# Cross attention and a mixture of experts: the first expert step in a new order, a token's rows by lower and higher expert, and products that nobody reads

## The reference

```python
x = x + cross_attention(layernorm(x), ctx, ctx, mask, Wq, bq, Wk, bk, Wv, bv, Wo, bo)   # 16 heads of 16
# flat: the 1792 rows (16 x 112) of layernorm(x), 256 wide
gate_probs = softmax(flat @ router_w)                       # 8 experts
topk_w, topk_idx = top_k(gate_probs, 2); topk_w /= topk_w.sum()
cw = zeros(T, 8).at[arange(T), topk_idx].add(topk_w)
h = silu(einsum('td,edf->etf', flat, w1))                   # 256 -> 512
y = einsum('etf,efd->etd', h, w2)                           # 512 -> 256
x = x + einsum('etd,te->td', y, cw)
```

## Time and profile before

| | |
|---|---|
| median of 3 runs | 491.9 us (490.89 to 492.44) |
| profiled execution | 491.83 us, its span 490.1 us |
| PE, DVE, ACT, POOL busy | 85%, 71%, 54%, 47% of the span |
| mean granted clock of TensorE | 0.917 |
| expert steps, first transposition to last output product | 326.6 to 465.9 |

### The profile page before, as it was taken

The page is one execution under the profiler, slowest core; times in us unless marked ns, Lnnn a source line. Parts: engine busy times, 40 slices in busy tenths (PEclk is TensorE's granted clock), DMA queues, the critical chain, the costliest instruction groups (busy, mean ns, idle before and its releaser), DMA issues.

```text
span 490.1 us, 10668 instructions
## 1 busy us (share of the span) xinstructions
PE 414.3 (85%) x4155; PEld 383.4 (78%) x4155; DVE 345.7 (71%) x703; ACT 266.4 (54%) x350; POOL 232.4 (47%) x263
## 2 busy tenths in 40 slices
PE   2475679999999999999999999637989999999800
PEld 2364557999999989999988988537989999999800
DVE  2785466887877878887787858854686666666427
ACT  3231226567566666557663453526767777777500
POOL 8352343422333222332222374753676888886443
PEclk9796689999999999999999997558999999999965
DMA  7949838777777778877641039912222222332157
GB/s 174 229 132 230 269 117 166 155 160 162 155 161 161 159 133 170 177 160 145 144 101 34 26 108 379 327 54 55 66 86 66 87 87 87 87 88 74 47 211 267
DMA packets 58323, 69.83 MB, mean 142 GB/s; under 512 B 19073, under 2 KB 51602, under 8 KB 58274
## 3 DMA queue, kind: packets, MB, share of 16 engines
q1 hardware_dynamic: 52338, 56.30, 47.5%
q0 software_dynamic: 4032, 11.02, 7.6%
q10 hardware_dynamic: 1904, 1.84, 1.1%
HBM read 35.64 MB, written 14.78 MB: 103 GB/s over the span
## 4 chain that ended last, share of the span: by engine, by line
PE 74%; DVE 11%; issue 5%; DMA 4%; ACT 3%; POOL 2%; DVEq 0%; SPq 0%; ACTq 0%; POOLq 0%
PE ps L1467 38%; PE ps L1528 11%; PE ps L1543 9%; PE ps L1557 8%; DVE x L1457 2%; PE ps L1817 2%; PE ps L1570 1%; DVE x_rows_sb L1100 1%; DVE neg_max L1053 1%; DMA y_back<-y_rows 1%; PE ps L1636 1%; DVE h_lo L1384 1%; PE ps L1638 1%; ACT h_hi L982 1%; DMA keep<-keep_scratch 1%
## 5 line engine op out<-in xcount | busy, mean ns | idle before, releaser
L1053 DVE TENSOR_REDUCE neg_max<-ps 112x1 f32<-112x376 f32 x256 | 133.7, 546 | 38.2 <-PE ps L1528 33.6
L830 ACT ACTIVATE probs<-ps 125x1344 f32<-125x1344 f32 x64 | 82.7, 1292 | 42.9 <-PE ps L1543 37.7
L1528 PE MATMUL ps<-k_stack,q_stack 98*112 98x376 f32 x256 | 88.1, 378 | 11.0 <-issue 6.5
L589 POOL TENSOR_TENSOR k_lo<-k_f,k_hi 128x752 fp32r<-128x752 f32 x16 | 28.8, 1801 | 120.2 <-ACT k_hi L804 117.7
L1528 PEld LDWEIGHTS ps<-k_stack,q_stack 98*112 98x112 f32 x256 | 45.2, 178 | 24.8 <-DVE neg_max L1053 14.0
L748 POOL DMA_INDIRECT rows<-xn_rows,token_of_row x42 | 53.9, 1284 | 20.6 <-issue 12.2
L756 POOL DMA_INDIRECT y_rows<-y_out,slot_of_row x42 | 45.3, 1078 | 33.4 <-ACT y_out L996 23.3
L1543 PE MATMUL ps<-q_stack,k_stack 100*125 100x224 f32 x384 | 52.8, 273 | 0.4 <-ACT probs L830 0.3
L1467 PE MATMUL ps<-flat_t_hi,w_hi 128*128 128x256 f32 x168 | 48.7, 290 | 4.5 <-DVE flat_t_lo L1362 4.5
L1543 PEld LDWEIGHTS ps<-q_stack,k_stack 100*125 100x125 f32 x384 | 50.5, 188 | 1.5 <-ACT probs L830 1.0
L1467 PE MATMUL ps<-w_hi,h_hi 128*128 128x256 f32 x168 | 48.6, 289 | 3.0 <-issue 1.6
(11 more groups left out here) (200 smaller groups left out, 1011.9 us busy)
## 6 DMA issues: line engine op xcount, KB each, us to landing
k_stack<-k_hi SPq DMA_DIRECT2D x64, 188.0 KB, 4.5
w_all<-w SPq DMA_DIRECT2D x2, 4096.0 KB, 18.0
k_stack<-k_lo SPq DMA_DIRECT2D x32, 188.0 KB, 5.5
ctx_raw<-ctx_t SPq DMA_DIRECT2D x32, 187.5 KB, 5.3
q_stack<-q_scratch SPq DMA_DIRECT2D x32, 168.0 KB
q_scratch<-q_hi SPq DMA_DIRECT2D x16, 224.0 KB, 3.1
y_back<-y_rows SPq DMA_DIRECT2D x7, 512.0 KB, 6.6
q_scratch<-q_lo SPq DMA_DIRECT2D x8, 224.0 KB, 2.8
```

The source lines that it names most:

```text
L589: pool.tensor_tensor(kl[:, :, :], kf[:, :, :], kh[:, :, :].bitcast(F32), ALU.subtract)\
L830: act.activation(pf[j % 2][:, :, :], ps[0:CT, BK_ST:BK_ST + KT, 0:4 * S], ACT.Exp).then_inc(pf_ready, 1)
L1053: dve.tensor_reduce(neg_max[:, s:s + 1], ps[0:S, BK_MAX + s % 2, 0:CP], AX.X, ALU.max, negate=True).then_inc(max_read, 1)
L1528: pe.matmul(ps[0:S, BK_MAX + a, 0:CP], qs[b.ring][0:R_MAX, q, S * a:S * (a + 1)], ks[b.ring][0:R_MAX, q, :], start=True, stop=True).then_i ...
```

## The change

In the planning, `chosen[:, 0]` becomes the expert with the lower number of a token's two, `chosen[:, 1]` the other. In the tail, outputs are loaded back in two halves: those of the lower experts once all steps but the last have been scattered (and the last `w1_low` is done, since they lie where `w1_all` was), then those of the higher experts; each half is seven transfers of 256 KB in pieces of 1 KB. DVE makes all 28 sums, POOL none. On ACT, `silu` splits in `silu` and `silu_high`, and the order in a step becomes silu(t), rows_high(t+1), silu_high(t), w2_high(t), copy_y(t-1), w1_high(t+2); a Silu of one column stands behind the gates' Exp. The first step has an order of its own on ACT, DVE and PE. PE makes 24 products into a bank that nobody reads ahead of the first transposition and 8 behind it.

```diff
+BK_SPIN = 3
...
-        y_back = sb("y_back", [P, NT, TOP, D])
+        y_back = sb("y_back", [P, TOP, NT, D])
...
-            for p in range(2):
-                sp.wait_ge(y_scattered[p], 32 * ((STEPS - p + 1) // 2))
-            for g in range(NTG):
-                sp.dma_start(y_back[:, 2 * g:2 * g + 2, :, :],
-                             y_rows[TOP + TOP * TG * g:TOP + TOP * TG * (g + 1), :]
-                             .rearrange("(n p c) d -> p n c d", p=P, c=TOP)).then_inc(y_in[g], 16)
+            def load_outputs(c):
+
+                steps_done = STEPS - 1 + c
+                for p in range(2):
+                    sp.wait_ge(y_scattered[p], 32 * ((steps_done - p + 1) // 2))
+                if c == 0:
+                    sp.wait_ge(w1l_ready, STEPS)
+                for g in range(NTG):
+                    sp.dma_start(y_back[:, c, 2 * g:2 * g + 2, :],
+                                 y_rows[TOP + TOP * TG * g:TOP + TOP * TG * (g + 1), :]
+                                 .rearrange("(n p c) d -> p c n d", p=P, c=TOP)[:, c, :, :]).then_inc(y_in[c][g], 16)
...
             def silu(t):
                 act.wait_ge(h_done, t.n + 1)
-
                 if not early(t, 2):
                     act.wait_ge(hl_ready, t.n - 1)
+                act.activation(hf[t.par][:, :, :], silu_source(t), ACT.Silu).then_inc(hf_ready, 1)
+
+            def silu_high(t):
+                if not early(t, 2):
                     act.wait_ge(y_done, t.n - 1)
...
             def step(t):
+                if is_step(t):
+                    silu(t)
                 if is_step(t.after(1)):
-                    w1_high(t.after(1))
                     rows_high(t.after(1))
                 if is_step(t):
-                    silu(t)
+                    silu_high(t)
                     w2_high(t)
                 if is_step(t.after(-1)):
                     copy_y(t.after(-1))
+                if is_step(t.after(2)):
+                    w1_high(t.after(2))
...
             act.activation(gates[2][:, :, :], gates[1][:, :, :], ACT.Exp).then_inc(gate_exp, 1)
+            act.activation(std[:, 0:1], eps_c[:, :], ACT.Silu)
             act.wait_ge(table_ready, 1)
-            for n in range(-1, STEPS + 1):
+            step_0 = Batch(0, 0)
+            w1_high(step_0)
+            w1_high(step_0.after(1))
+            rows_high(step_0)
+            w2_high(step_0)
+            rows_high(step_0.after(1))
+            silu(step_0)
+            silu_high(step_0)
+            w1_high(step_0.after(2))
+            for n in range(1, STEPS + 1):
                 step(Batch(0, n))
...
-                dve.tensor_scalar(picked[:, tiles, :], order[:, tiles, :], 0.0, None, ALU.is_equal)
-                step(dve.tensor_scalar(second[:, tiles, :], order[:, tiles, :], 1.0, None, ALU.is_equal))
+                step(dve.scalar_tensor_tensor(out=marked[:, tiles, :], in0=order[:, tiles, :], scalar=1.0,
+                                              in1=pos[:, tiles, :], op0=ALU.is_le, op1=ALU.mult))
+                step(dve.tensor_reduce(c3[:, tiles], marked[:, tiles, :], AX.X, ALU.max))
+                step(dve.tensor_tensor(lower[:, tiles, :], marked[:, tiles, :], wide2(c3, tiles), ALU.is_equal))
+                step(dve.tensor_tensor(upper[:, tiles, :], both[:, tiles, :].bitcast(F32), lower[:, tiles, :],
+                                       ALU.subtract))
...
             def expert_step(t):
-                after = t.after(1)
-                if is_step(after):
-                    w1_low(after)
-                    rows_low(after)
+                if is_step(t.after(1)):
+                    rows_low(t.after(1))
                 if is_step(t):
                     h_low(t)
                     w2_low(t)
+                if is_step(t.after(2)):
+                    w1_low(t.after(2))
...
-            for n in range(-1, STEPS + 1):
+            step_0 = Batch(0, 0)
+            w1_low(step_0)
+            w1_low(step_0.after(1))
+            rows_low(step_0)
+            w2_low(step_0)
+            rows_low(step_0.after(1))
+            h_low(step_0)
+            w1_low(step_0.after(2))
+            for n in range(1, STEPS + 1):
                 expert_step(Batch(0, n))
                 if n == 3:
                     weigh()
...
+            def spin(times):
+
+                for n in range(times):
+                    pe.matmul(ps[:, BK_SPIN, 0:2 * P], earlier[:, :], is_place[:, 0, 0:2, :], start=True, stop=True)
...
-            for n in range(-1, STEPS + 1):
+            step_0 = Batch(0, 0)
+            spin(24)
+            rows_transpose(step_0)
+            spin(8)
+            hidden(step_0, range(0, 1))
+            rows_transpose(step_0.after(1))
+            hidden(step_0, range(1, KF))
+            for n in range(1, STEPS + 1):
                 step(Batch(0, n))
```

More of the change, by code:

```diff
@@ L91, in lanes_of @@
     return [(c, n) for c in range(TOP) for n in tiles]
[L94 to L99, removed]
 class Batch:
@@ L259, in xattn_moe_kernel @@
         cursor["at"] = late_start
-        y_back = sb("y_back", [P, NT, TOP, D])
-        assert cursor["at"] <= weights_end, "the outputs come back where the experts' raw weights were"
+        y_back = sb("y_back", [P, TOP, NT, D])
+        assert cursor["at"] <= late_start + 4 * E * KD * F, "the outputs come back where the experts' first raw weights were"
         cursor["at"] = weights_end
@@ L553, in _ @@
                 write_rows(u)
-            for p in range(2):
-                sp.wait_ge(y_scattered[p], 32 * ((STEPS - p + 1) // 2))
-            for g in range(NTG):
-                sp.dma_start(y_back[:, 2 * g:2 * g + 2, :, :],
-                             y_rows[TOP + TOP * TG * g:TOP + TOP * TG * (g + 1), :]
-                             .rearrange("(n p c) d -> p n c d", p=P, c=TOP)).then_inc(y_in[g], 16)
+            def load_outputs(c):
[8 more added lines that the diff above has]
+                                 .rearrange("(n p c) d -> p c n d", p=P, c=TOP)[:, c, :, :]).then_inc(y_in[c][g], 16)
+            for c in range(TOP):
+                load_outputs(c)
             sp.wait_ge(out_written, 16 * NTG)
@@ L1231, in read_logits @@
                                   .rearrange("p (n h e) -> p n e h", h=2, e=E), AX.X, ALU.add).then_inc(logits_read, 1)
-            logits, shifted, expd, rest, t0, t1, cw = gates
-            picked, second = chosen[:, 0, :, :], chosen[:, 1, :, :]
+            logits, shifted, expd, marked, t0, t1, cw = gates
+            lower, upper = chosen[:, 0, :, :], chosen[:, 1, :, :]
             c0, c1, c2, c3 = gcol
@@ L1449, in _ @@
                     weigh()
-            for g in range(NTG):
-                dve.wait_ge(y_in[g], 16)
-                for c in range(TOP):
+            for c in range(TOP):
+                for g in range(NTG):
+                    dve.wait_ge(y_in[c][g], 16)
                     if c:
-                        dve.wait_ge(first_added, adds_to(g))
-                    for n in dve_adds(g):
-                        dve.scalar_tensor_tensor(out=x2[:, n, :], in0=y_back[:, n, c, :], scalar=weight[:, c, n:n + 1],
+                        dve.wait_ge(lower_added, 2 * (g + 1))
+                    for n in range(2 * g, 2 * g + 2):
+                        dve.scalar_tensor_tensor(out=x2[:, n, :], in0=y_back[:, c, n, :], scalar=weight[:, c, n:n + 1],
                                                  in1=x2[:, n, :], op0=ALU.mult, op1=ALU.add)\
-                            .then_inc((first_added, out_ready)[c], 1)
+                            .then_inc((lower_added, out_ready)[c], 1)
         @block.tensor
@@ L1819, in rows_transpose, with hidden @@
                 last.then_inc(rt_done, 1)
-            def hidden(t):
+            def hidden(t, parts=range(KF)):
                 pe.wait_ge(rl_ready, t.n + 1)
@@ L1826, in hidden @@
                     pe.wait_ge(hh_ready, t.n - 1)
-                for f in range(KF):
+                for f in parts:
                     c = slice(f * P, (f + 1) * P)
@@ L1831, in hidden @@
                                     for w, x in ((w1h, fh), (w1l, fh), (w1h, fl))])
-                last.then_inc(h_done, 1)
+                if KF - 1 in parts:
+                    last.then_inc(h_done, 1)
             def expert_out(t):
```

33 lines of the change are left out of this document (8 added, 25 removed).

## The result

The changed kernel takes 485.54 us in the median of 4 runs (484.36 to 485.80), against 492.17 (4 runs, 490.89 to 492.64) for the kernel before on the same chip: ratio 0.9865, 95% interval 0.9839 to 0.9890, or 6.6 us faster. The forecast was 11.4 us faster, 480.5, with a range up to 484.8: the sign was right, the size was not, and the result lies outside the range. A second measurement, beside the kernel before on another chip, gave 485.67 (6 runs) and a ratio of 0.9862. The ratios compare fast runs; one run of the kernel before, beside x5 to x8, took 1003.07 us and is left out.

A forecast was written before the change was run, and what follows sets the result against it. TensorE was taken to bound the expert stage without a gap, leaving entry, weighing and tail. Span 490.1 - 5.0 (planning's +0.45 included) - 1.0 - 5.3 = 478.8, with 1.7 around the span 480.5 us; range 478.0 to 484.8.

The forecast's parts named there:

- Planning: In `find_two`, two overlapped operations become four: +0.45 us up to the gathers (bounds 0 to 1.3), the late half hidden.
- Clock: At the entry, spare products bring TensorE from half to full speed by about 326, before step 0's products; worth 2.3 us.
- Rival 1: At the entry, the clock does not rise during the spare products: +1.0 to +2.3 us, together 482; 15%.
- Entry: From gathers to first output product: it starts at 336.0 and not 341.03, -5.0 us (bounds -2.7 and -5.7).
- Early Silu: On ACT, a dummy Silu moves the 1.28 us table load into the wait for the step table, hiding it.
- Rival 4: On ACT, the table load is placed at the first silu again: +1.3 us, 481.8; 3%.
- Steady order: In each expert step, ACT's new order costs nothing, hidden by the output products; margin 0.85 us.
- Weighing: At the gate weights after step 3, TensorE stalls 0.6 us for 1.67: -1.0 (bounds 0 and -1.7).
- Rival 3: In every step, rows come late: 486 at 0.3 us over, 492 and more from 0.6; 5% some loss, 2% slower.
- Tail: After the last product, loads in halves and DVE sums end the span at 484.8: -5.3 us (bounds -5.5 and -2.5).
- rival 2: In the tail, early loads delay step 20's scatters by 1 to 2 us: tail -2.5, 483.3; 15%.
- The sum: Whole kernel: span 490.1 - 5.0 - 1.0 - 5.3 = 478.8, forecast time 480.5 us, 11.4 us faster.

The follow-up runs named there:

- x5: Changed kernel without the eight spare products behind the first transposition and without hidden products ahead of the second: 487.95 us, one run.
- x8: Changed kernel with three of the first seven output loads behind step 19's scatter, the others behind step 20's: 486.18 us, ratio 0.9870.
- x2: Kernel before with only the spare products added (24 ahead of the first transposition, 8 behind it): 489.67 us, ratio 0.9952.
- x4: Changed kernel with step 1's `w1_low` put behind step 0's `rows_low` on VectorE: 486.0 us, ratio 0.9878.
- x11: Changed kernel without the scatter of step 20's outputs, all fourteen loads following step 19's scatter: 483.42 us, median of 2, ratio 0.9802.
- x13: Changed kernel with its 24 and 8 spare products made 12 and 4 of twice the width: 483.6 us, ratio 0.9831.
- x16: x13 measured again, beside the changed kernel on one chip: 484.78 us of 6 runs, ratio 0.9844.
- x9: Changed kernel without the early Silu that nobody reads ahead of the step table: 486.42 us, one run.
- x17: Changed kernel measured and profiled again, unchanged: 485.67 us of 6 runs, ratio 0.9862.
- x18: Kernel before run once more, unchanged, for a second profile: 493.31 us, one run.
- x3: Changed kernel with all output loads started behind step 20's scatter, none early: 486.97 us, ratio 0.9887.
- x1: Changed kernel without its 32 spare products: 486.66 us, ratio 0.9895.
- x6: x5 with both `w1_low` put behind `rows_low` on VectorE: 487.93 us, one run.

## Why the prediction was right or wrong, point by point

- *Planning* (+0.45): the four operations took 1.03 us where 0.93 was taken, but the stretch up to the token list changed by 0.0 in the mean of two profiles, inside its variation. The cover of the late half held.
- *Clock*: right in place and size (rise at 326.0; 2.5 us alone, x2). Rival 1 did not come in the changed kernel's two profiles, but it is near: of the eight profiles with TensorE's order as in the changed kernel, the clock fell again during the entry in two, x4 and x11, and x11's entry is 1.5 us longer for it. The rival had priced it at +1.0 to +2.3.
- *Entry* (-5.45 behind the planning): -4.4. The step that failed is "the later gather lands 2.7 to 3.6 later, 3.1 in the median". That median was taken from gathers of before, where the instruction packet comes at 337.86, far behind step 1's rows. Here it lay on this gather, whose last mark came 4.4 behind the start and not 3.1; clear of the packet it is 3.2 to 3.4 with the same gather of 1.51. With it moved (x13, x16) the entry is 14.7 to 14.8, and the forecast had 14.6. The sum was right; a transfer in it was not alone on its transfer engine.
- *Early Silu* (hides 1.28): the load was hidden, but it would have been anyway (x9). Rival 4's price was wrong too.
- *Steady order* (0): right, TensorE has no gap there. *Weighing* (-1.0): -0.9, stall 0.75 for the 0.6 worked out. Rival 3 is out.
- *Tail* (-5.3): -3.4 in the two profiles, -2.7 in the mean of all with this tail. The step that failed is "the second half still starts when step 20 has landed, 470.45": the landing itself took 2.6 to 3.3 us more because of the loads that the change sends ahead of it. This is rival 2, with its 15%; I priced the delay at 1 to 2 us and the tail at -2.5, and the delay was larger. The size of the loss is not far from the rival's: -2.7 against -2.5. x11 gives the cost of the collision, 1.7 to 2.4, and confirms the rest. The forecast noted that loads would be in flight and still added a landing time from a row where the queues were empty.
- *The sum*: tail 1.9 and entry 1.1 make 3.0 of the 4.8 us that the forecast was too good; with the tail's mean of twelve profiles it is 3.7. The terms as measured in the two profiles, -4.4, -0.9 and -3.4, make -8.7; less the 1.0 by which the early mark came later in the mean of two, that is, to a tenth or two, the 7.9 by which the spans' means (490.85 and 483.0) differ. The medians differ by 6.6 and 6.1 only. Part of this gap is which executions were profiled: x17's profile is of the fastest of its six runs, 1.8 us under their median, and x18's 493.31 lies 1.5 above the median of its neighbours (491.78). Executions of one kernel lie 1.1 to 5.4 us apart in these measurements, and part of that is the start, ahead of all edits (early marks from 299.5 to 302.0). What of the last 1 to 2 us is such chance stays open.

Both failures have one form: a transfer was priced as if its transfer engines were free. The Trainium skill, "DMA: Bandwidth & Descriptors", section Queues, rings and completion order, says that a transfer's semaphore write lands only after every earlier write of the same transfer engine, whatever queue it came from. That rule holds up the mark of bytes that have moved already. The traces show more than that, the bytes themselves late. The late packet of the gather moved from 331.70 to 332.14, where the others had ended by 331.43: 0.7 of the 1.15 us by which its mark trails; whether the rule accounts for the rest no run tells. The data packets of step 20's second scatter move 1.5 to 1.9 us behind its start in x3, where nothing is queued, and 3.3 to 5.1 behind it in the changed kernel, between those of the loads (the lists of queues, x3 in 465.10 to 465.60 and the changed kernel in 468.35 to 470.25; the scatters start at 463.63 and 465.11):

```profile
q0 software_dynamic: 42, 0.13, 73.8%
```
```profile
q1 hardware_dynamic: 548, 0.53, 82.5%
q0 software_dynamic: 47, 0.13, 17.2%
```

## What to carry to other kernels

When a change starts transfers earlier, don't reuse the landing times of those that now go out behind them: take the bytes queued in front into the sum, and ask which landing releases the second batch. When a stream waits for a small transfer at a critical point, look at the list of queues in that window for packets that are not its own; an instruction packet moves with the number of instructions ahead of it. Here 16 wide filler products in place of 32 narrow ones, with the same columns, kept the clock and moved the packet off the critical transfer. And when a part is taken out to learn its worth, as the spare products in x1, check in the trace what else moved with it. And profile the unchanged kernel twice before a mark in front of the edit is read as an effect.

## What the runs showed of the hardware that was not expected

- One 16 KB packet of the instruction queue, 0.96 to 1.4 us on one transfer engine, holds back one sixteenth of an indirect gather of 128 KB, and with it the gather's landing, by 0.7 to 1.2 us (nine profiles; 1.1 in the changed kernel). Taking 16 products out ahead of it moved it from 0.25 us ahead of step 0's first hidden product to 3.1 (x13) and 2.6 us (x16) behind it. That it is TensorE's code is inferred from this.
- An indirect scatter of 128 KB lands in 2.4 us alone and in 5.0 to 5.8 behind 1.8 MB of queued loads (twelve profiles). Its data packets wait, not only its completion.
- ScalarE loads a table before it waits for the data of the activation that needs it (x9: load at 333.86 to 335.14, its data there at 335.3).
- An indirect gather costs GpSimd 1.51 us and not 0.94 while VectorE makes a low part (x5, x6).
- TensorE's clock fell from 1.00 to 0.50 in x4 behind 1.79 us without work, and in x11 at 332.38, where the waits before it were 1.17 and 0.94 us. It stayed at 1.00 in the changed kernel behind waits of 1.43 and 1.02. So the longest single wait does not tell whether it falls.
